# Eight 32x32 tiles in two PSUM banks for the last 26 keys of an attention, and one division for a whole unit

## The chip, the cores and the metric

One core of one Trainium2 chip runs the whole program. The metric is the device time of one execution in microseconds (us); 2626.75 us is the median of three runs of the kernel before.

## The reference

Four layers follow each other over an input of 4 batches of 1024 rows of 256 values. Each layer is a cross attention to 154 context rows ("keys"), then a feed-forward part. The attention of layers 1 to 3 has 16 heads of 16 values; layer 0 calls the same kind of attention with the layer's normalised rows as queries, feature maps of 32 values a head and its own output weight.

```python
x = x + tanh(g_xattn[l]) * xattn_l(layernorm(x), ctx_1024, ...)
x = x + tanh(g_ffn[l]) * ffn_l(layernorm(x), ...)
# inside an attention
scores = einsum('bhqd,bhkd->bhqk', q, k) / sqrt(d_k)
attn = softmax(scores, axis=-1)
x = einsum('bhqk,bhkd->bhqd', attn, v)
```

The feed-forward parts are a butterfly network folded into two matrices (layer 0), a linear layer with a top-2 low-rank choice (1), a ternary network with quantised activations (2) and a gated mixture with low-rank experts (3).

## The kernel before

The rows of a batch are cut into four blocks of 256; a stream `s` (0 to 3) takes one block through all layers, so that four independent streams share the engines. One attention of one stream in one layer `l` and batch is called a unit here: there are 16 units of layer 0 and 48 of layers 1 to 3. Every engine works through a fixed list of stages. A planner in the kernel (`orders`) makes the five lists: for each turn it takes the stream that a table of digits names (`TURN`, one string for each engine), and uses a cost for each stage (`parts`) to give out PSUM banks and to find gaps of TensorE of over 0.9 us, into which it puts `fill` matmuls that compute nothing (L982).

PSUM has 8 banks of 128 partitions x 512 fp32 values. Banks 0 to 3 form `quad`, for the scores. Banks 4 to 7 are handed out one at a time; `take(k)` makes TensorE wait until the engine that last read bank `k` is done.

The stages of a unit that matter here, in their order, each with its TensorE lines:

- `sc` and `mx` find the row maxima (L1136 to L1149), `mt` turns them.
- `st` (layer 0, L1175 and L1178) and `sts` (the others, L1196 and L1198) give the transposed scores of the last 26 keys, whose exponentials ScalarE writes to `s.Et`, which is stored in the buffers `xn` and `xT`. Layer 0 has two `st`, one for each half unit `u`, of one bank each.
- `s2` (L1219, L1222) and `ex` (ScalarE, L1585) give the exponentials `ET` of the first 128 keys, for one half unit at a time.
- `pv` multiplies them with the values. Its helper `through` does 8 matmuls of 128 keys (L1239, four column tiles of 32) and then 8 of the last 26 keys (L1247, 32x32 tiles whose row group and column group have the same number, into one bank). In layer 0 `pz` does the same with ones in place of the values, into a second bank: these are the sums of the softmax. In layers 1 to 3 the sums stand in unused columns of the values.
- `no` and `nz` divide: VectorE transposes the bank in 32x32 blocks (L1859), takes reciprocals (L1876) and transposes these back, spread over their heads (L1878); ScalarE copies the bank (L1601); GpSimd multiplies (L924) and adds (L926). All of it is done once for each half unit.
- `out` multiplies with the output weight (L1288).

```python
for q in range(4):
    t = e.matmul(bank[G4[q], 256 * z:256 * z + 256], last(z, q), Et[G4[q], 256 * a:256 * a + 256],
                 start=False, stop=True, skip_group_check=True)
```

Of the kernel before, what the change touches and what calls it, by code (L numbers as in the profile page):

```python
# [29 lines left out]
def build(nc, d, out):  # L30
# [5 lines left out]
    with ctx:  # L36
# [11 lines left out]
        ones = sb("ones", [128, 128])  # L48
# [130 lines left out]
        for i in range(NS):  # L179
# [3 lines left out]
            s.xn = sb(f"xn{i}", [128, 2, 256])  # L183
            s.xT = sb(f"xT{i}", [128, 2, 256])
# [6 lines left out]
            s.z = sb(f"z{i}", [128, 16])  # L191
# [41 lines left out]
            s.Et = [s.flat, xTf]  # L233

# [3 lines left out]

            s.PW = [s.flat, gu[:, 2048:2560], part(1536, [512])]
# [11 lines left out]

        def xrows(s, b):
            return slice(1024 * b + 256 * s.i, 1024 * b + 256 * s.i + 256)
# [3 lines left out]
        def parts(name, of):  # L257
            l = of[2] if name in ("qp", "sc", "s2", "ex", "pv", "pz", "no", "nz", "out", "split") else 0
            u = of[-1] if name in ("ex", "no") else 0
            key0 = name == "key" and of[1] == 0  # L260
            pe = {"grow": (150, 150, 250, 450, 880, 880, 880)[of[-1]] if name == "grow" else 0, "near": 450, "upt": 560, "tsum": 110, "key": 600 if key0 else 1150, "val": 1500, "turn": 600,
                  "qp": 910 if l == 0 else 1830, "sc": (740, 980, 740, 1280)[l], "mt": 220, "st": 1200,
                  "sts": 2500 if name == "sts" and of[2] == 3 else 1600, "s2": (1400, 1400, 1400, 2300)[l], "pv": 2000,
                  "pz": 2000, "out": 3550 if l == 0 else 1850, "up": 1800, "down": 7050, "gate1": 2150, "tl": 350,
# [3 lines left out]
                   "val": 850, "norm": 1750, "mx": 1390, "no": 1800 if l == 0 else 750, "nz": 950, "out": 770,  # L268
# [4 lines left out]
                   "turn": 600, "qp": 600 if l == 0 else 760, "mt": 350, "st": 500, "sts": 1100, "ex": 1800, "pv": 560,  # L273
                   "up": 860, "gate1": 200, "gate3": 200, "tl": 400, "q1": 500, "gelu2": 4400, "q2": 1000, "rd": 2400, "mw": 600,
                   "h1": 360, "h2": 360, "norm": 1000, "no": 900}
            pool = {"split": 1500, "key": 1500, "mw": 1650, "norm": 2600, "bias": 1550, "hw": 2050,
                    "no": 1250, "nz": 2350}
# [5 lines left out]
                   "split": "G", "no": "dg" if l == 0 else "Da", "nz": "dg", "pv": "PA" if l == 0 else "P",  # L283
# [11 lines left out]
        ONE = ("tsum", "key", "val", "turn", "qp", "mt", "st", "sts", "pv", "pz", "out", "up", "down", "gate1", "tl", "q1", "w1",  # L295
               "q2", "w2", "gate3", "mw", "exa", "h1", "f3")
        READ = {"tern": "DVE", "key": "ACT", "val": "DVE", "turn": "ACT", "qp": "ACT", "mt": "ACT", "st": "ACT", "sts": "ACT", "no": "DVE", "out": "DVE",
# [3 lines left out]
        def takes(name, of, engine):  # L301
# [4 lines left out]
            if (name, engine) == ("mw", "POOL") and of[1] == 0:  # L306
                return ["gated"]
            if engine == "PE" and (name in ONE or name == "back" and of[1] == 0):
# [1949 lines left out]
```

## Time and profile before

| | before |
|---|---|
| median of 3 runs | 2626.75 us (2623.39 to 2628.63) |
| profiled execution, span | 2625.2 us (no other time of it is listed) |
| TensorE busy | 2472.9 us, 94% |
| VectorE, ScalarE, GpSimd busy | 57%, 46%, 45% |
| TensorE's share of the chain that ended last | 74% |
| granted TensorE clock, mean | 0.992 |
| DMA | mean 14 GB/s |

The span is from the first to the last instruction. A fp32 matmul leaves two records in the trace, a bf16 matmul one, so 8 fp32 matmuls are "x16". The names are those of the program's buffers.

### The profile page before, as it was taken

To read this page: it belongs to the slowest core of one execution; us is meant where nothing else is said; L and a number is where in the kernel's file an instruction comes from. 1 tells how busy PE (TensorE), PEld (TensorE's weight loads), DVE (VectorE), ACT (ScalarE), POOL (GpSimd) and SP (SyncE) were. 2 spreads that over 40 slices of the span, in tenths; PEclk is the share of its full clock that TensorE was granted. 3 is DMA by queue.
4 is the path that set the end of the run, shared out by engine and by line. 5 is a ranking of instruction groups with operands and counts; after the bars stand their busy time and mean duration, and the time that the engine had idled before them with its cause. 6 is when DMAs were issued, how large, how long until landed. Compare 5 with 4: busy or idle time off the path is not lost.

```text
span 2625.2 us, 53630 instructions
## 1 busy us (share of the span) xinstructions
PE 2472.9 (94%) x21300; PEld 1670.9 (64%) x21300; DVE 1491.8 (57%) x3948; ACT 1204.5 (46%) x1930; POOL 1170.3 (45%) x2521
## 2 busy tenths in 40 slices
PE   8999888999999988899999998899999999889998
PEld 5676445777776644577777655467767765447776
DVE  7555787545433687754543467874543257876442
ACT  5535477322244547723224546762322545674221
POOL 2334644545343554444533355444534345545442
PEclk9999999999999999999999999999999999999999
DMA  3200100000000000000000000000000000000000
GB/s 130 84 12 12 76 14 2 1 9 9 9 9 12 12 1 14 2 6 12 1 9 20 1 12 1 12 1 9 9 9 9 12 1 12 1 1 1 5 5 9
DMA packets 16279, 37.37 MB, mean 14 GB/s; under 512 B 1408, under 2 KB 11424, under 8 KB 15008
## 3 DMA queue, kind: packets, MB, share of 16 engines
q1 hardware_dynamic: 16032, 33.94, 3.7%
q8 instruction: 172, 2.82, 0.5%
q14 instruction: 75, 0.61, 0.1%
HBM read 29.74 MB, written 4.19 MB: 13 GB/s over the span
## 4 chain that ended last, share of the span: by engine, by line
PE 74%; DVE 14%; ACT 5%; POOL 4%; issue 3%; DMA 0%; DVEq 0%; POOLq 0%; ACTq 0%
PE P L1431 8%; PE P L1239 4%; PE P L1247 4%; PE P L1140 4%; PE P L1464 4%; PE P L1440 4%; PE P L1449 4%; PE P L1313 4%; PE P L1432 4%; PE P L1300 4%; PE P L1288 4%; PE P L1219 4%; DVE mx L1849 4%; ACT ET L1585 2%; PE P L1109 2%
## 5 line engine op out<-in xcount | busy, mean ns | idle before, releaser
L1849 DVE TENSOR_REDUCE mx<-P 128x8 f32<-128x1232 f32 x256 | 367.7, 1436 | 195.8 <-PE P L1136 63.5
L872 POOL TENSOR_SCALAR sm<-sm 128x1 f32<-128x1 f32 x512 | 174.6, 353 | 457.9 <-DVE sm L1845 457.4
L1431 PE MATMUL P<-xT,w 128*128 128x256 f32 x1024 | 265.6, 382 | 1.5 <-DVE sm L2042 0.8
L1543 ACT ACTIVATE xn<-x,sm 128x256 f32<-128x256 f32 x256 | 139.5, 593 | 228.3 <-POOL sm L878 228.2
L1885 DVE SCALAR_TENSOR_TENSOR x<-P,w_first,x 128x512 f32<-128x512 f32 x96 | 71.9, 749 | 290.7 <-PE P L1465 109.1
L1431 PEld LDWEIGHTS P<-xT,w 128*128 128x128 f32 x1024 | 190.3, 190 | 51.7 <-issue 25.9
L1585 ACT ACTIVATE ET<-P 128x2048 f32<-128x2048 f32 x96 | 180.1, 1876 | 68.1 <-PE P L1222 46.4
L1663 ACT ACTIVATE gu<-P 128x256 f32<-128x256 f32 x128 | 49.0, 383 | 331.1 <-PE P L1432 311.0
L1140 PE MATMUL P<-KB,R 32*128 32x308 f32 x1536 | 156.5, 476 | 39.0 <-ACT ET L1585 16.2
L2072 DVE SCALAR_TENSOR_TENSOR gu<-gu,P 128x256 f32<-128x256 f32 x128 | 53.7, 419 | 215.9 <-ACT gu L1663 215.6
L1219 PE MATMUL P<-R,KB 32*128 32x256 f32 x2048 | 162.3, 403 | 8.3 <-DVE mx L1849 8.3
L1239 PE MATMUL P<-ET,VB 128*32 128x256 f32 x2048 | 137.0, 385 | 20.4 <-ACT ET L1585 15.2
L1432 PE MATMUL P<-gu,b 128*128 128x256 f32 x512 | 152.3, 379 | 0.0
L889 POOL TENSOR_TENSOR x<-x,w_bias 128x512 f32<-128x512 f32 x112 | 142.0, 1271 | 18.8 <-ACT xn L1543 18.8
L924 POOL TENSOR_TENSOR xT<-xT,R 128x512 f32<-128x512 f32 x48 | 61.0, 1272 | 184.3 <-DVE xT L1878 113.4
L877 POOL TENSOR_SCALAR sm<-sm 128x1 f32<-128x1 f32 x512 | 132.0, 272 | 24.5
L1440 PE MATMUL P<-gu,b 128*128 128x256 f32 x512 | 133.8, 384 | 0.0
L1140 PEld LDWEIGHTS P<-KB,R 32*128 32x128 f32 x1536 | 62.1, 185 | 101.6 <-issue 59.0
L950 POOL TENSOR_TENSOR xn<-xn,gu 128x512 f32<-128x512 f32 x48 | 60.9, 1270 | 145.0 <-DVE xn L2079 143.8
L1300 PE MATMUL P<-xT,wup 128*128 128x256 f32 x512 | 124.1, 387 | 0.4 <-ACT R L1609 0.4
L1219 PEld LDWEIGHTS P<-R,KB 32*128 32x128 f32 x2048 | 81.3, 186 | 65.4 <-issue 34.4
L1464 PE MATMUL P<-w_w,R 128*128 128x256 f32 x512 | 116.6, 381 | 3.4 <-issue 3.0
(310 smaller groups left out, 5583.7 us busy)
## 6 DMA issues: line engine op xcount, KB each, us to landing
kvw<-in_wkv SPq DMA_DIRECT2D x12, 672.0 KB, 4.0
x<-in_x SPq DMA_DIRECT2D x16, 256.0 KB, 2.9
out<-x SPq DMA_DIRECT2D x16, 256.0 KB, 2.1
w<-in_w SPq DMA_DIRECT2D x2, 1024.0 KB, 6.3
w<-in_wexp SPq DMA_DIRECT2D x1, 1028.0 KB, 7.8
w_w<-in_wcon SPq DMA_DIRECT2D x1, 1024.0 KB, 10.1
w_w<-in_m3t SPq DMA_DIRECT2D x1, 1024.0 KB, 8.6
w<-in_w1q SPq DMA_DIRECT2D x1, 1024.0 KB, 10.6
```

The lines of the kernel that those rows point to most:

```text
L872: own(e.tensor_scalar(a[:, i:i + 1], y[:, i:i + 1], y[:, i:i + 1], hv[:, i:i + 1], ALU.mult, ALU.mult), 1)
L889: e.tensor_tensor(s.x[:], s.x[:], gb[:, k:k + 1, :].broadcast_to([128, 2, 256]), ALU.add).then_inc(s.g_x, 1)
L1140: t = e.matmul(quad[:, g, 0:2 * NK], s.QT[G4[g], u, rows], K[G4[g], 2 * u:2 * u + 2, :], start=True, stop=l == 2)
L1219: e.matmul(quad[:, g, cols], K[G4[g], j, 0:128], s.QT[G4[g], j if l == 0 else u, :], start=a == 0, stop=False, skip_group_check=True)
L1239: t = e.matmul(bank[G4[q], 256 * z:256 * z + 256], main(z, q), ET[:, g, 256 * a:256 * a + 256], start=z == 0, stop=False, skip_group_check ...
L1300: t = e.matmul(o[:, 256 * (j % 2):256 * (j % 2) + 256], wup[:, c, 128 * j:128 * j + 128], s.xT[:, c, :], start=c == 0, stop=c == 1)
L1431: e.matmul(o, wm[:, c, js], s.xT[:, c, :], start=n == c == 0, stop=False, skip_group_check=True)
L1432: t = e.matmul(o, bm[:, js], U[:, 2 * n, :], start=False, stop=False, skip_group_check=True)
L1440: t = e.matmul(P[:, k, 256 * n:256 * n + 256], bm[:, js], U[:, 2 * n + 1, :], start=False, stop=n == 1, skip_group_check=True)
L1464: e.matmul(o, s.G[:, j, rows], w2[:, j, :], start=j == 0, stop=False)
L1585: e.activation(ET[:].rearrange("p g c -> p (g c)"), quad.rearrange("p g c -> p (g c)"), ACT.Exp, bias=mb1[:, b:b + 1] if l == 1 else 0.0). ...
L1849: e.tensor_reduce(s.mx[:, i, :, 2 * u:2 * u + 2], quad[:, :, 0:2 * NK].rearrange("p g (a k) -> p g a k", a=2), AX.X, ALU.max).then_inc(q_d, 1)
```

## The change

- The exponentials of the last 26 keys lie in one buffer `s.Et` of 128 x 2 x 512, whose halves `xn` and `xT` now are. Instruction rows of the changed kernel therefore say `Et` for all three.
- `st` is one stage for the whole unit of layer 0, into two banks. For each `u`, eight tiles follow each other, four with row group = column group in the first bank (`z` = 0), four with the row group 2 further on in the second bank (`z` = 1).
- `last` writes the product of the last 26 keys in the same way: row group `q` for `z` = 0, `q ^ 2` for `z` = 1, always column group `q`. In layer 0, `pv` does values and ones side by side in the two banks, and `pz` is gone. In layers 1 to 3, `pv` of `u` = 0 does only the first 128 keys; `pv` of `u` = 1 does its own, and then the last 26 keys of both half units as one block of 16 matmuls. The two banks are taken at `u` = 0 and kept.
- The division is done once for a unit of layers 1 to 3: two transposes, two reciprocals and one transpose back, a scaled copy of one bank by ScalarE, a multiply-add of the other bank by VectorE, one multiply by GpSimd. Bias rows and value columns are laid out anew to suit.
- `both` joins two neighbouring banks in one instruction of ScalarE or VectorE.
- The strings of `TURN` are all new, and the planner's costs of the stages above too.

```diff
-            s.xn = sb(f"xn{i}", [128, 2, 256])
-            s.xT = sb(f"xT{i}", [128, 2, 256])
+            s.Et = sb(f"Et{i}", [128, 2, 512])
+            s.xn, s.xT = (s.Et[:, z, :].rearrange("p (a b) -> p a b", a=2) for z in range(2))
...
+        def both(k0, k1):
+            k0, k1 = sorted((k0, k1))
+            if k1 == k0 + 1:
+                return [(slice(0, 2), P[:, k0:k0 + 2, :])]
+            return [(slice(z, z + 1), P[:, k:k + 1, :]) for z, k in enumerate((k0, k1))]
...
-                "0323230023233232020102202102220102210000331000333101333021211212111021212302123023201321222032322013"
...
-            def nz(s, b, l, u):
-                t = s.Z[u]
-                e.wait_ge(s.d_o, C.up(s.d_o))
-                e.wait_ge(s.a_q, 13 * b + 3 * l + 3 + u)
-                e.tensor_tensor(t, t, s.VS, ALU.mult).then_inc(s.g_z, 1)
-                e.wait_ge(s.g_z, C.up(s.g_z))
-                e.tensor_tensor(s.OT[:, u, :], t[:, 0:256], t[:, 256:512], ALU.add).then_inc(s.g_p, 1)
+            def nz(s, b, l):
+                e.wait_ge(s.d_o, C.up(s.d_o, 2))
+                e.tensor_tensor(s.OT[:, 0:2, :].rearrange("p a b -> p (a b)"), s.Z[0], s.VS, ALU.mult).then_inc(s.g_p, 1)
                 C.up(s.g_p)
...
-            def st(s, b, u, k):
+            def st(s, b, k0, k1):
                 K = KT[0]
...
+                k0, k1 = sorted((k0, k1))
                 banks = take(k0), take(k1)
...
                 for u in range(2):
...
+                    eight = [(g, z, banks[z][G4[g ^ 2 * z], 256 * u:256 * u + 256]) for z in range(2) for g in range(4)]
+                    for g, z, o in eight:
+                        e.matmul(o, K[G4[g], 2 * u + z, :], s.QT[G4[g], 2 * u + z, :], start=u == 0, stop=False,
+                                 skip_group_check=True)
+                    for g, z, o in eight:
+                        t = e.matmul(o, selt[G4[g], 2 * u + z, :], s.MT[G4[g], :], start=False, stop=True, skip_group_check=True)
...
+            def last(s, l, u, z, o, of):
+
+                for q in range(4):
+                    r = G4[q ^ 2 * z]
+                    t = e.matmul(o[G4[q], :], of[r, :], s.Et[r, z, 256 * u:256 * u + 256], start=False, stop=True, skip_group_check=True)
                 return t
...
                 if l == 0:
...
+                    for z, o in enumerate(banks):
+                        main(s, 0, u, z, o[:, half[0]], lambda q, z=z: V[:, 8 * u + 4 * z + q, :], True)
+                        t = main(s, 0, u, z, o[:, half[1]], lambda q: ones[:, 0:32], False)
+                    t.then_inc(p_et, 1)
+                    if u == 0:
+                        e.wait_ge(s.a_e, s.e)
+
+                    for z, o in enumerate(banks):
+                        last(s, 0, u, z, o[:, half[0]], Vt[:, 2 * u + z, :])
+                    for z, o in enumerate(banks):
+                        t = last(s, 0, u, z, o[:, half[1]], one26[:])
                     t.then_inc(s.p_d, 1)
...
+                for z, o in enumerate(banks):
+                    t = main(s, l, u, z, o[:, half[u]], lambda q, z=z: V[:, 8 * u + 4 * z + q, :], u == 0)
+                t.then_inc(p_et, 1)
+                if u == 0:
+                    return
+                e.wait_ge(s.a_e, s.e)
+
+                for n in range(2):
+                    for z, o in enumerate(banks):
+                        t = last(s, l, n, z, o[:, half[n]], Vt[:, 2 * n + z, :])
+                t.then_inc(s.p_d, 1)
...
+            def no(s, b, l, k0, k1):
+
+                e.wait_ge(s.d_a, C.up(s.d_a, 2) - 1)
+                e.activation(s.VS, P[:, k0, :], ACT.Copy, scale=tm[:, 2:3]).then_inc(s.a_q, 1)
...
+                for n in range(2):
+                    e.reciprocal(z[:, :, n], s.Z[n].rearrange("p (b c) -> p b c", c=32)[:, :, 16 - 16 * n]).then_inc(d_own, 1)
                 e.wait_ge(d_own, C.up(d_own, 2))
-                e.transpose(t, s.z[:].unsqueeze(2).broadcast_to([128, 16, 32])).then_inc(s.d_o, 1)
+                e.transpose(s.Z[0], z.unsqueeze(3).broadcast_to([128, 16, 2, 16])).then_inc(s.d_o, 1)
+                e.wait_ge(s.a_q, 10 * b + 2 * l + 4)
+                e.scalar_tensor_tensor(out=s.VS, in0=P[:, k1, :], scalar=tm[:, 3:4], in1=s.VS, op0=ALU.mult,
+                                       op1=ALU.add).then_inc(s.d_o, 1)
```

The first place is TensorE in the first units of layer 0 of the kernel before: the second `st`, then `pv` and `pz` of one half unit.

```order
L1175 MATMUL P<-R,KT 32x256 x4
L1178 MATMUL P<-R,selt 32x256 x4
L1175 MATMUL P<-R,KT 32x256 x4
L1178 MATMUL P<-R,selt 32x256 x4
L1018 MATMUL P<-b,w_b1q 128x256 x2
L1136 MATMUL P<-KB,R 128x154 x8
L1239 MATMUL P<-ET,VB 32x256 x8
L1247 MATMUL P<-xn,VR 32x256 x8
L1239 MATMUL P<-ET,ones 32x256 x8
L1247 MATMUL P<-xn,one 32x256 x8
```

In the changed kernel TensorE has there one `st`, and further on one `pv` for the same half unit.

```order
L1173 MATMUL P<-R,KT 32x256 x8
L1176 MATMUL P<-R,selt 32x256 x8
L1173 MATMUL P<-R,KT 32x256 x8
L1176 MATMUL P<-R,selt 32x256 x8
L1016 MATMUL P<-b,w_b1q 128x256 x2
```

```order
L1134 MATMUL P<-KB,R 128x154 x8
L1236 MATMUL P<-ET,VB 32x256 x4
L1236 MATMUL P<-ET,ones 32x256 x4
L1236 MATMUL P<-ET,VB 32x256 x4
L1236 MATMUL P<-ET,ones 32x256 x4
L1243 MATMUL P<-Et,VR 32x256 x8
L1243 MATMUL P<-Et,one 32x256 x8
```

The number of matmuls is the same; those of the last 26 keys (L1247 before, L1243 now) stand in one block of 16 where two blocks of 8 stood, and the changes of tile shape between L1239 and L1247 are one in place of three.

The second place is TensorE in the first units of layer 1. Before, each half unit ends with its own block of the last 26 keys.

```order
L1300 MATMUL P<-xT,wup 128x256 x4
L1239 MATMUL P<-ET,VB 32x256 x8
L1247 MATMUL P<-xn,VR 32x256 x4
L1247 MATMUL P<-xT,VR 32x256 x4
L1087 MATMUL P<-ident,xn 128x128 x4
L1219 MATMUL P<-R,KB 128x256 x4
L1222 MATMUL P<-R,sel 128x256 x4
L1219 MATMUL P<-R,KB 128x256 x4
L1222 MATMUL P<-R,sel 128x256 x4
```

Now the first half unit has none, and the second has both.

```order
L1156 MATMUL P<-identb,R 128x128 x2
L1236 MATMUL P<-ET,VB 32x256 x8
L1217 MATMUL P<-R,KB 128x256 x4
L1220 MATMUL P<-R,sel 128x256 x4
L1217 MATMUL P<-R,KB 128x256 x4
L1220 MATMUL P<-R,sel 128x256 x4
L1107 MATMUL P<-Et,w_wq 128x256 x4
L1236 MATMUL P<-ET,VB 32x256 x8
L1243 MATMUL P<-Et,VR 32x256 x16
```

The block of 8 behind the first L1239 has moved behind the second one and joined the block there.

The third place is VectorE's division in layer 1, before for two half units and now for one unit.

```order
L1859 STREAM_TRANSPOSE R<-P 128x512
L1876 RECIPROCAL z<-R 128x8 x2
L1878 STREAM_TRANSPOSE R<-z 128x512
L1859 STREAM_TRANSPOSE xT<-P 128x512
L1876 RECIPROCAL z<-xT 128x8 x2
L1878 STREAM_TRANSPOSE xT<-z 128x512
```

```order
L1884 STREAM_TRANSPOSE R<-P 128x512
L1884 STREAM_TRANSPOSE Et<-P 128x512
L1900 RECIPROCAL z<-R 128x16
L1900 RECIPROCAL z<-Et 128x16
L1902 STREAM_TRANSPOSE R<-z 128x512
L1904 SCALAR_TENSOR_TENSOR R<-P,w_first,R 128x512
```

Both transposes of PSUM now stand together, one transpose back is gone, and a multiply-add out of PSUM has come behind it. Over the whole program the lists hold 296 `fill` matmuls before and 309 now; GpSimd has 144 tensor-tensor instructions less, ScalarE 160 activations less and 2 table loads more.

## Rows read from the trace of the kernel before

**Rows 1.** The page: busy time by engine, and the chain that ended last.

```profile
PE 2472.9 (94%) x21300; PEld 1670.9 (64%) x21300; DVE 1491.8 (57%) x3948; ACT 1204.5 (46%) x1930; POOL 1170.3 (45%) x2521
PE 74%; DVE 14%; ACT 5%; POOL 4%; issue 3%; DMA 0%; DVEq 0%; POOLq 0%; ACTq 0%
```

**Rows 2.** Busy time by stretch, first and last of four equal stretches.

```profile
100.00:700.00 600.00, 562.55 (x5017) 377.39 (x5016) 357.03 (x934) 287.70 (x450) 269.63 (x594) 0.99 0.05 16
...
1900.00:2500.00 600.00, 571.38 (x5043) 384.75 (x5035) 338.67 (x900) 277.63 (x438) 269.23 (x575) 1.00 0.02 6
```

**Rows 3.** Timeline of TensorE, layer 0, `st`: start, duration, instruction, records.

```profile
70.47 0.63 PE L1175 MATMUL P<-R,KT 32*32 32x256 f32 x8
70.92 0.29 PE L1178 MATMUL P<-R,selt 32*32 32x256 bf16 x4
71.03 0.61 PE L1175 MATMUL P<-R,KT 32*32 32x256 f32 x8
71.47 0.29 PE L1178 MATMUL P<-R,selt 32*32 32x256 bf16 x4
71.68 0.71 PE L1219 MATMUL P<-R,KB 32*128 32x256 f32 x8
```

**Rows 4.** Timeline of TensorE, layer 0, `pv` and `pz` of one half unit.

```profile
75.37 1.07 PE L1239 MATMUL P<-ET,VB 128*32 128x256 f32 x16
76.37 1.06 PE L1247 MATMUL P<-xn,VR 32*32 32x256 f32 x16
77.36 1.07 PE L1239 MATMUL P<-ET,ones 128*32 128x256 f32 x16
78.36 1.07 PE L1247 MATMUL P<-xn,one 32*32 32x256 f32 x16
79.36 0.71 PE L1219 MATMUL P<-R,KB 32*128 32x256 f32 x8
...
80.66 3.72 PE L1288 MATMUL P<-w_fcw,R 128*128 128x256 f32 x16
84.22 0.60 PE L1087 MATMUL P<-ident,xn 128*128 128x128 f32 x4
```

**Rows 5.** Timeline of TensorE, layer 2, both `pv` of one unit.

```profile
351.04 1.07 PE L1239 MATMUL P<-ET,VB 128*32 128x256 f32 x16
...
360.52 1.07 PE L1239 MATMUL P<-ET,VB 128*32 128x256 f32 x16 [0.63 <-ACT ET L1585]
361.52 0.63 PE L1247 MATMUL P<-xn,VR 32*32 32x256 f32 x8
361.98 0.61 PE L1247 MATMUL P<-xT,VR 32*32 32x256 f32 x8
362.51 0.80 PE L1140 MATMUL P<-KB,R 32*128 32x308 f32 x8
```

**Rows 6.** Groups of TensorE: records, busy us and mean ns, idle before.

```profile
L1239 PE MATMUL P<-ET,VB 128*32 128x256 f32 x2048 | 137.0, 385 | 20.4 <-ACT ET L1585 15.2 <-issue 4.1
L1247 PE MATMUL P<-xn,VR 32*32 32x256 f32 x1024 | 77.9, 385 | 0.0
L982 PE MATMUL P<-identb 128*128 128x512 bf16 x296 | 77.7, 389 | 4.5 <-POOL mg L839 4.5
```

**Rows 7.** Groups of the division and the residual, on the other engines.

```profile
L1859 DVE STREAM_TRANSPOSE R<-P 128x512 f32<-128x512 f32 x48 | 34.2, 713 | 24.0 <-PE P L1247 24.0
L1878 DVE STREAM_TRANSPOSE R<-z 128x512 f32<-128x512 f32 x48 | 34.1, 711 | 1.7
L1885 DVE SCALAR_TENSOR_TENSOR x<-P,w_first,x 128x512 f32<-128x512 f32 x96 | 71.9, 749 | 290.7 <-PE P L1465 109.1 <-PE P L1313 98.5 <-PE P L1288 78.4
L1876 DVE RECIPROCAL z<-R 128x8 f32<-128x8 f32 x96 | 13.1, 178 | 1.0
L1601 ACT ACTIVATE R<-P,w_first 128x256 f32<-128x256 f32 x192 | 80.3, 472 | 80.6 <-DVE R L1859 42.6 <-DVE xT L1859 33.8 <-POOL R L924 3.8
L924 POOL TENSOR_TENSOR R<-R 128x512 f32<-128x512 f32 x48 | 60.9, 1269 | 68.4 <-DVE R L1878 42.3 <-ACT R L1601 26.1
L926 POOL TENSOR_TENSOR R<-R 128x256 f32<-128x256 f32 x48 | 35.0, 728 | 3.8
```

More of the change, by code:

```diff
@@ L307, in takes @@
                 return ["gated"]
+            if (name, engine) == ("pv", "PE") and of[2] > 0 and of[3] > 0:
+                return []
             if engine == "PE" and (name in ONE or name == "back" and of[1] == 0):
-                return ["bank"] * (2 if name in ("sts", "gate1") else 1)
+                return ["bank"] * (2 if name in ("st", "sts", "gate1", "pv") else 1)
             return []
@@ L314, in gives @@
                 return ["quad"]
-            if engine == "PE" and (name == "pz" or name == "pv" and of[2] > 0):
+            if (name, engine) == ("pv", "PE"):
                 return ["ET"]
-            if (name, engine) == ("pv", "ACT") or (READ.get(name) if name != "no" or of[2] == 0 else "ACT") == engine:
-                return ["bank", "gated"] if name == "e3" else ["bank"] * (2 if name in ("sts", "lin") else 1)
+            if (name, engine) in (("pv", "ACT"), ("nz", "DVE")) or READ.get(name) == engine and (name != "no" or of[2]):
+                return ["bank", "gated"] if name == "e3" else ["bank"] * (2 if name in ("st", "sts", "lin", "pv") else 1)
             return []
@@ L627, in build @@
+            "SP": "0300030102300000123000001230002103",
         }
@@ L1193, in sts @@
                 for u in range(2):
-                    o = [banks[g // 2][64 * (g % 2):64 * (g % 2) + 64, 256 * u:256 * u + 256] for g in range(4)]
+                    o = [banks[g // 2][64 * h:64 * h + 64, 256 * u:256 * u + 256] for g, h in enumerate((0, 1, 1, 0))]
                     for g in range(4):
@@ L1851, in mx, with pv, no @@
                 C.up(q_d)
-            def no(s, b, l, u, k):
-                t, bank = s.Z[u] if l else s.Et[u], P[:, k, :]
+            def pv(s, b, l, u, k0, k1):
+                e.wait_ge(s.p_d, C.up(s.p_d))
+                for z, of in both(k0, k1):
+                    t = e.transpose(s.Et[:, z, 256 * u:256 * u + 256], of[:, :, 256:512])
+                t.then_inc(s.d_a, 1)
+                C.up(s.d_a)
+            def no(s, b, l, *at):
                 C.up(s.g_p)
-                e.wait_ge(s.p_d, C.up(s.p_d))
@@ L1858, in no @@
                 if l:
[L1859 to L1860 removed]
+                    e.wait_ge(s.p_d, C.up(s.p_d))
+                    for z, k in enumerate(at):
+                        e.transpose(s.Z[z], P[:, k, :]).then_inc(s.d_a, 1)
+                    C.up(s.d_a, 2)
                     return
[L1862 to L1864 removed]
```

318 lines of the change are left out of this document (147 added, 171 removed).

## The prediction, before the changed kernel had run

> **What bounds the kernel now.** I read the page first. TensorE is busy for 2472.9 of 2625.2 us, no other engine for more than 57%, and TensorE has 74% of the chain that ended last [rows 1]. Then the stretches: between 100 and 2500 us TensorE is busy for 563 to 571 of every 600 us [rows 2], so it is idle for 29 to 37 us in each. The kernel is bound by TensorE, evenly, with about 152 us of idle time in all (2625.2 - 2472.9). Some of the busy time is not work: 77.7 us are `fill` matmuls, which stand where the planner expects a gap [rows 6]. A microsecond of real TensorE work that goes away is a microsecond of time, as long as the gaps don't grow.
>
> Last I read the timeline of the stages that are changed, by the starts of the pieces, since the ends overlap. A block of 8 fp32 matmuls of the last 26 keys (L1247, 16 records) runs from 76.37 to 77.36, 1.00 us; the block of the 128 keys ahead of it (L1239) takes 1.00 us as well [rows 4]. What is in that microsecond? Two blocks of one tile shape that follow each other show it: the second L1175, 8 records, takes 71.47 - 71.03 = 0.44 us, and the first L1178, 4 records, 0.11 us [rows 3]. Full-array fp32 matmuls of 256 columns take 3.56 us for 16 records [rows 4], 0.22 us each. So four records of 32x32 tiles together take what one full-array record takes: the four tiles run at the same time, in groups of 0.216 us. A block of 16 records is four such groups, 0.864 us, and 0.136 us for the change of tile shape.
>
> **The change part by part.** The price of a block now hangs on one question: do the four tiles of the second bank run beside the four of the first? They have row groups of their own kind in the order (`q ^ 2`), so all eight tiles are different ones. No row shows eight tiles at once. The nearest rows on one side are the four at once of L1247; on the other, L1219, 32x128 tiles, four row groups that write all columns of four banks: its 8 records last 0.71 us in all, with the drain [rows 3], where one at a time would need 8 x 0.216 = 1.73 us. There the whole array is at work at once, and each column group serves four row groups; nothing in the rows forbids eight 32x32 tiles in two banks. The bounds are 1.03 us for 32 records, if all eight overlap, and 1.86 us (8 groups and a change of shape), if the second bank's four wait. I take full overlap: a group of eight records costs 0.216 us, and I allow 0.03 us a block for the four more starts. A block of 32 records is then 4 x 0.216 + 0.136 + 0.03 = 1.03 us.
>
> - Layers 1 to 3, last 26 keys: two blocks of 1.00 us [rows 4, 5] become one of 1.03: 0.97 us less, 48 units: 46.6 us.
> - Layer 0, last 26 keys: `pv` and `pz` of a half unit, 2 x 1.00, become one block of 1.03. Two half units in each of 16 units: 32 x 0.97 = 31.0 us.
> - Layer 0, the 128 keys: two blocks of 1.00 us now follow each other, one change of shape less: 32 x 0.136 = 4.4 us.
> - `st`: one stage is 71.68 - 70.47 = 1.21 us [rows 3], two are 2.42 us. The new one has the same four pieces, each of eight tiles: 1.21 + 0.03 = 1.24. Saved 1.18 x 16 = 18.9 us.
> - `sts`, `s2`, `sc`: the same tiles and counts, nothing.
>
> The sum is 100.9 us of TensorE work less, 4%.
>
> **The other engines.** In layers 1 to 3 GpSimd did 1.27 + 0.73 us for each half unit and now does 1.27 once: 2.73 us less a unit, 131 us over 48. ScalarE did four copies of 0.47 and does one of twice the width, between 0.47 and 0.94; at 0.6 it is 4 x 0.47 - 0.6 = 1.28 a unit, some 60 us less. VectorE loses a transpose of 0.71 and gets a multiply-add of 0.75 [rows 7]: nothing. So none of them comes nearer to being the bound. What gets longer is the tail of a unit, from TensorE's last product to `out`: before 0.71 + 2 x 0.18 + 0.71 + 1.27 + 0.73 = 3.8 us, now 2 x 0.71 + 0.36 + 0.71 + 0.75 + 1.27 = 4.5 us [rows 7]. Behind it waits `out` of that stream and everything that TensorE has in its list behind `out`. It costs nothing while the three other streams' work stands between; that cover is the 9.5 us between the two `pv` of a unit, which is other streams' work too [rows 5]. If it were gone everywhere it would cost 0.7 x 48 = 34 us. The new `last` block also waits for nothing that was not there: `s.Et` is older by a half unit than before.
>
> **The gaps.** By its code the planner fills 0.6 of a gap that it expects, and counts 0.215 us for a fill matmul. 13 more of them mean 13 x 0.215 / 0.6 = 5 us more of expected gaps. That is the only trace of the new order in numbers, and I add 5 us. 2626.75 - 100.9 + 5 = 2530.9; the span of the profiled execution is 1.6 us under the median and would give 2529. I say 2530 us.
>
> **A rule against it.** Four tiles of L1247 lie in four row groups and write one bank, and they take 0.216 us together [rows 3, 4]. The Trainium skill, TensorEngine Tiling (Array Packing), Restrictions and Gotchas, says that different row tiles can't access the same PSUM bank at the same time. Taken as it stands, the 16 records of a block before would need 16 x 0.216 = 3.5 us and the 32 now at least that. The row of 1.00 us contradicts it for tiles that also differ in their column group, as all do within one bank here. The same skill, TensorE: Matmul & The Clock Gate, Part 3, tells of 16 tiles of 32x32 at 10.6 times the speed of one; no row here shows more than four 32x32 tiles.
>
> **The rivals.** (a) *The second bank's tiles wait for the first's.* Each column group then serves one tile at a time. For it speaks that no row has two tiles of one column group in flight at this tile size; against it, L1219, where four row groups share all columns. Then only changes of shape are saved: 0.136 us for 80 joined blocks, 4.4 us in the 128 keys, 0.1 us for each of 16 `st`: 17 us, so 2626.75 - 17 + 5 = 2615 us. (b) *They overlap by half*: the second four start one record late, since a matmul's second record queues ahead of them. A block then needs five groups in place of four, and so does each piece of `st`: 0.216 x (80 + 32) = 24 us back: 2555 us. (c) *The waits take part of it*: the longer tail at its full 34 us, or waits for a bank: 2545 to 2590, about 2565 us. (d) *Slower: banks.* In layers 1 to 3 two of the four single banks are now held from the first `pv` to the multiply-add: in the unit shown, 9.5 us between the `pv` [rows 5] plus 1.0 + 1.0 + 3.2, about 15 us, where one bank was held for a few us at a time. Two units that overlap hold all four, and every `take` behind them (`turn`, `qp`, `mt`, `up`) stands until VectorE is through. It decides from 101 / 48 = 2.1 us a unit; at 3 us it gives 2530 + 144 = 2674 us. For it speaks that TensorE's list can't go around a stage that waits; against it, that the planner hands out these same banks and would have shown such waits as gaps, hence as fills, and there are only 13 more. (e) *The new order is better by itself*, with idle time down by 20 us or more: 2505 us.
>
> **How the numbers follow.** Forecast 0.68, (a) 0.05, (b) 0.07, (c) 0.12, (d) 0.03, (e) 0.05. A measurement of this kernel can't tell less than about 0.2%, 5 us, from no change; every case but (d) is faster by more, and I leave 0.01 for no change, between (a) and (d). Faster 0.96, same 0.01, slower 0.03. The forecast's own spread is the gaps, -15 to +20 us: 2515 to 2550. The range takes in (b), the lower half of (c) and part of (e): 2510 to 2560 us.
>
> **What the profile of the changed kernel would show.** L1243: a block of 32 records from start to the next line's start in about 1.03 us (1.25 with (b), 1.9 with (a)), and a busy time for each 1024 records of about half of the 77.9 us that they have now [rows 6]. L1173 with 16 records in about 0.46 us. TensorE busy at about 2375 us, the idle time at 150 to 160 us. GpSimd busy some 130 us less. If idle time is at 190 us or more, with L1236 or the stages behind a `take` waiting for VectorE's multiply-add, (c) or (d) is at work. I am wrong if the block takes much over 1.1 us, or if the waits before `out` and `take` have grown by more than 20 us.

## The result: less than half of the forecast gain

The changed kernel takes 2584.66 us (median of 4 runs, 2579.62 to 2586.76), the kernel before 2625.97 us (4 runs, 2623.39 to 2628.63) on the same chip. The ratio is 0.9839, 95% interval [0.9824, 0.9853]: 41 us faster, where 97 were forecast. 2584.66 lies outside the forecast's 2510 to 2560 us. The profiled execution of the changed kernel took 2586.76 us, its span is 2585.0 us and its mean granted TensorE clock 0.980; before, the clock was 0.992 over 2625.2 us.

The page of the changed kernel, busy time and chain, answers to [rows 1]. The third row is the granted clock in 40 slices, in tenths; before the change all 40 digits were 9.

```profile
PE 2398.4 (93%) x21282; PEld 1654.5 (64%) x21313; DVE 1451.4 (56%) x3871; ACT 1162.8 (45%) x1772; POOL 1036.9 (40%) x2377
...
PEclk9999899999999999999999988999999999899999
...
PE 69%; DVE 15%; ACT 7%; issue 5%; POOL 4%; DMA 1%; SPq 0%; DVEq 0%; POOLq 0%; ACTq 0%
```

By this page TensorE is busy 74.5 us less (forecast 98), and idle for 186.6 us in place of 152.3; 6.5 us of both are not real, as the ledger below says. TensorE's share of the chain fell from 74% to 69%; ScalarE's and "issue" grew. GpSimd is busy 133 us less, as forecast (130). ScalarE has 42 us less (60 forecast): the old copies overlapped, 192 of 0.472 us in 80.3 us [rows 7], the new ones take 0.68 us each, and there are two table loads more. VectorE has 40 us less (nothing forecast); it is spread over many small groups, and its cause was not looked for.

The timeline of TensorE, for layer 0 and for layer 2, answers to [rows 3 to 5]: start, duration, instruction, records, idle time before.

```profile
48.06 0.66 PE L1173 MATMUL P<-R,KT 32*32 32x256 f32 x16
48.51 0.31 PE L1176 MATMUL P<-R,selt 32*32 32x256 bf16 x8
...
55.94 0.61 PE L1236 MATMUL P<-ET,ones 128*32 128x256 f32 x8
56.48 0.66 PE L1243 MATMUL P<-Et,VR 32*32 32x256 f32 x16
56.94 0.64 PE L1243 MATMUL P<-Et,one 32*32 32x256 f32 x16
57.51 0.71 PE L1217 MATMUL P<-R,KB 32*128 32x256 f32 x8
```

```profile
359.01 0.80 PE L1138 MATMUL P<-KB,R 32*128 32x308 f32 x8 [0.84 <-ACT R L1583]
359.74 1.07 PE L1236 MATMUL P<-ET,VB 128*32 128x256 f32 x16
360.74 1.09 PE L1243 MATMUL P<-Et,VR 32*32 32x256 f32 x32
361.76 0.61 PE L980 MATMUL P<-identb 128*128 128x512 bf16 x2
```

Read the starts. The 32 records of L1243 take 361.76 - 360.74 = 1.02 us, and 57.51 - 56.48 = 1.03 us in layer 0: all eight tiles run at once. L1173 with 16 records takes 48.51 - 48.06 = 0.45 us, as 8 records did. So TensorE does have what the sum said. The time is not there.

**The ledger.** Where did it go? I split each span into three: the idle time of the page (span less PE's busy time); what the lower clock costs, (1 - granted clock) x span; and the rest, TensorE's work at full clock, fills included. The middle term is exact only if TensorE works all through a stretch at half clock; in the changed kernel it was busy for 92 of 102 us of such stretches. The ratio of each run is to runs of the kernel before that were made beside it. Each split is that of the kernel's own profiled execution.

Nine of these traces lack records of TensorE. The page shows it: 21282 matmuls beside 21313 weight loads in the changed kernel, where the kernel before has 21300 of both. All 31 are missing from one group, which has 128 records in e3 and e4:

```profile
L1388 PE MATMUL P<-w1i,Et 128*128 128x512 bf16 x97 | 33.2, 399 | 9.2 <-ACT Et L1648 4.8 <-issue 2.2 <-ACT R L1583 0.5
```

A block of two such records lasts 0.59 us and a single one 0.38, so each missing record takes 0.21 us out of "work" and puts it into "idle": 6.5 us for 31. The table has the numbers of the pages as they are, and the last column says how many records are missing; the text below puts the 6.5 us back (5 us in e6). With that, after, e4, e5 and e9, whose work is the same, agree within 3 us, and before and e6 within 6.

| kernel | time, ratio to before | span | work | clock | idle | missing records |
|---|---|---|---|---|---|---|
| before | 2625.97 | 2625.2 | 2451.9 | 21.0 | 152.3 | 0 |
| after | 2584.66, 0.9839 | 2585.0 | 2346.7 | 51.7 | 186.6 | 31 |
| e1 before, bf16 halves | 2584.94, 0.9836 | 2579.7 | 2349.1 | 38.7 | 191.9 | 0 |
| e2 after, bf16 halves | 2548.33, 0.9698 | 2545.2 | 2303.4 | 40.7 | 201.1 | 0 |
| e3 after, four at a time | 2642.42, 1.0056 | 2640.0 | 2436.8 | 29.0 | 174.2 | 0 |
| e4 after, short tail | 2569.45, 0.9778 | 2569.1 | 2353.7 | 41.1 | 174.3 | 0 |
| e5 after, short norm | 2540.45, 0.9668 | 2537.2 | 2345.7 | 27.9 | 163.6 | 31 |
| e6 before, short norm | 2597.14, 0.9882 | 2595.0 | 2440.9 | 18.2 | 135.9 | 24 |
| e7 after, no fills | 2605.59, 0.9915 | 2602.2 | 2274.9 | 80.7 | 246.6 | 31 |
| e8 after, 0.9 filled | 2576.31, 0.9801 | 2580.2 | 2385.7 | 43.9 | 150.6 | 31 |
| e9 after, norm in pairs | 2565.6, 0.977 | 2563.8 | 2348.4 | 33.3 | 182.1 | 31 |
| e10 after, bf16, 0.9 filled | 2552.17, 0.9718 | 2548.8 | 2336.6 | 38.2 | 174.0 | 30 |
| e11 e10 and pairs | 2539.09, 0.9667 | 2538.5 | 2333.0 | 43.2 | 162.3 | 30 |
| e12 e2 and short norm | 2506.3, 0.9537 | 2502.4 | 2291.7 | 35.0 | 175.7 | 30 |

After against before, with the missing records put back: work -99 (forecast -101), clock +31 (not forecast), idle +28 (forecast +5).

**The clock.** The term that was not forecast can be read in one place. The timeline of TensorE and the granted clock (the last but two numbers of a window's row) around 1590 us of the changed kernel:

```profile
1577.40 0.61 PE L1195 MATMUL P<-R,KT 32*64 32x256 f32 x8
1577.84 0.29 PE L1197 MATMUL P<-R,selt 32*64 32x256 bf16 x4
...
1583.98 0.71 PE L1217 MATMUL P<-R,KB 32*128 32x256 f32 x8 [0.46 <-DVE mx L1868]
...
1587.41 0.80 PE L1138 MATMUL P<-KB,R 32*128 32x308 f32 x8 [2.06 <-ACT ET L1608]
1588.14 1.36 PE L1236 MATMUL P<-ET,VB 128*32 128x256 f32 x16
1589.43 1.96 PE L1243 MATMUL P<-Et,VR 32*32 32x256 f32 x32
1592.98 0.61 PE L1353 MATMUL P<-ident,R 128*32 128x128 f32 x2 [1.60 <-ACT R L1622]
...
1600.08 1.07 PE L1195 MATMUL P<-R,KT 32*64 32x256 f32 x8
1600.93 0.43 PE L1197 MATMUL P<-R,selt 32*64 32x256 bf16 x4
```

```profile
1575.00:1588.00 13.00, 10.06 (x126) 5.81 (x124) 9.46 (x35) 5.26 (x5) 3.45 (x9) 1.00 0.00 0
1588.80:1602.50 13.70, 10.21 (x83) 4.14 (x80) 9.38 (x29) 4.21 (x8) 5.75 (x13) 0.50 0.00 1
1603.00:1616.00 13.00, 10.67 (x94) 6.21 (x87) 8.09 (x28) 12.10 (x13) 6.08 (x20) 1.00 0.00 0
```

TensorE waited 0.46 us for VectorE's row maxima (L1217, at 1583.98) and then 2.06 us for ScalarE's exponentials, and at 1588.8 us the clock fell to 1.2 GHz (0.50) for 13.7 us. The same block of L1195 takes 0.44 us ahead of it and 0.85 us in it. The Trainium skill, TensorE: Matmul & The Clock Gate, Part 1, gives 1.2 GHz for the "cold" array, its lower level, at which matmuls follow each other at half the pace; these rows agree. The kernel before has a like place at 1616 to 1630 us: TensorE waited for 1.03 us for the row maxima and then 1.87 us for the exponentials, with five fills in between where the changed kernel has none, and was busy for 9.90 of the 14 us. The clock stayed at 1.00. So waits of this length come before the fall, but they don't always bring it.

What is such a term worth in time? Executions of one and the same kernel differ in their clock. Of the 32 executions of the kernel before that were made beside e1 to e12, one had a clock of 0.993 and 2622.47 us, another 0.987 and 2635.42: 13 us for a clock term that differs by 16. A line through all 32 gives 0.76 us of span for each us of the term; 54 executions of the other kernels, each against the mean of its own, give 0.59. By that estimate the 31 us are worth 18 to 23 us of time. It is an estimate, because the gaps of these executions are not known.

### The profile page after: what moved, and what is told of

It reads as the page before. It is cut to its first block, busy times and chain, and to the rows that moved or that the text cites. A ratio compares the mean times of both kernels' runs of the same rounds, so it can differ in the third digit from the quotient of the medians.

```text
span 2585.0 us, 53036 instructions
## 1 busy us (share of the span) xinstructions
PE 2398.4 (93%) x21282; PEld 1654.5 (64%) x21313; DVE 1451.4 (56%) x3871; ACT 1162.8 (45%) x1772; POOL 1036.9 (40%) x2377
## 4 chain that ended last, share of the span: by engine, by line
PE 69%; DVE 15%; ACT 7%; issue 5%; POOL 4%; DMA 1%; SPq 0%; DVEq 0%; POOLq 0%; ACTq 0%
PE P L1451 9%; PE P L1484 4%; PE P L1236 4%; PE P L1452 4%; PE P L1469 4%; PE P L1460 4%; PE P L1333 4%; PE P L1217 4%; DVE mx L1868 4%; PE P L1320 4%; PE P L1138 4%; PE P L1308 3%; ACT ET L1608 3%; PE P L1243 2%; PE P L1107 2%
## 5 line engine op out<-in xcount | busy, mean ns | idle before, releaser
L873 POOL TENSOR_SCALAR sm<-sm 128x1 f32<-128x1 f32 x512 | 170.9, 344 | 520.0 <-DVE sm L1864 519.6
L1451 PE MATMUL P<-Et,w 128*128 128x256 f32 x1024 | 264.5, 381 | 0.3 <-DVE gu L2093 0.3
L1451 PEld LDWEIGHTS P<-Et,w 128*128 128x128 f32 x1024 | 191.7, 190 | 54.7 <-issue 26.1
L1563 ACT ACTIVATE Et<-x,sm 128x256 f32<-128x256 f32 x256 | 139.2, 593 | 182.7 <-POOL sm L879 182.6
L923 POOL TENSOR_TENSOR R<-R 128x512 f32<-128x512 f32 x48 | 61.2, 1274 | 323.2 <-DVE R L1904 323.1
L1217 PE MATMUL P<-R,KB 32*128 32x256 f32 x2048 | 171.4, 422 | 4.2 <-DVE mx L1868 4.1
L1236 PE MATMUL P<-ET,VB 128*32 128x256 f32 x2048 | 146.0, 391 | 23.0 <-ACT ET L1608 12.4
L1452 PE MATMUL P<-gu,b 128*128 128x256 f32 x512 | 152.3, 379 | 0.0
L1217 PEld LDWEIGHTS P<-R,KB 32*128 32x128 f32 x2048 | 85.3, 195 | 63.3 <-issue 39.3
L1320 PE MATMUL P<-Et,wup 128*128 128x256 f32 x512 | 124.8, 389 | 0.0
L947 POOL TENSOR_TENSOR Et<-Et,gu 128x512 f32<-128x512 f32 x48 | 60.9, 1269 | 155.2 <-DVE Et L2106 155.2
```

Of the source, the lines that this page charges most:

```text
L873: own(e.tensor_scalar(a[:, i:i + 1], y[:, i:i + 1], y[:, i:i + 1], hv[:, i:i + 1], ALU.mult, ALU.mult), 1)
L1217: e.matmul(quad[:, g, cols], K[G4[g], j, 0:128], s.QT[G4[g], j if l == 0 else u, :], start=a == 0, stop=False, skip_group_check=True)
L1236: t = e.matmul(o[G4[q], :], of(q), ET[:, g, 256 * a:256 * a + 256], start=start, stop=False, skip_group_check=True)
L1320: t = e.matmul(o[:, 256 * (j % 2):256 * (j % 2) + 256], wup[:, c, 128 * j:128 * j + 128], s.xT[:, c, :], start=c == 0, stop=c == 1)
L1451: e.matmul(o, wm[:, c, js], s.xT[:, c, :], start=n == c == 0, stop=False, skip_group_check=True)
L1452: t = e.matmul(o, bm[:, js], U[:, 2 * n, :], start=False, stop=False, skip_group_check=True)
```

## The experiments

Theory A, the prediction's own: TensorE bounds, so that its work is worth its full time, and what was missed came in with the new order, the longer tail or the banks. Theory B: the chains of the four streams through VectorE, GpSimd and ScalarE bound part of the time, so that TensorE's work is worth less than its time in any order. Theory C: gaps lower TensorE's clock, and that costs a part. Ratios are those of the table; intervals stand with each run.

**e1: TensorE's saving alone, in the kernel before.** Order, banks, tail and the other engines stay.

```diff
-    t = e.matmul(bank[G4[q], 256 * z:256 * z + 256], last(z, q), Et[G4[q], 256 * a:256 * a + 256],
+    hi = lambda x: x.bitcast(bf16).rearrange("p (n h) -> p n h", h=2)[:, :, 1]
+    t = e.matmul(bank[G4[q], 256 * z:256 * z + 256], hi(last(z, q)), hi(Et[G4[q], 256 * a:256 * a + 256]),
```

> The kernel before, its order, its banks and its division untouched; only the matmuls of the last 26 keys (L1247) read the upper halves of the fp32 numbers as bf16, so the numbers lose digits. TensorE work: a block of 16 records of 0.216 us by fours becomes 8 records of 0.109 us by fours, 0.65 us less for each of 160 blocks, 103 us less in all, about what the change took away. Theory A (TensorE work is worth its full time; the new order, the longer tail or the held banks gave the gain back): about 2523 us. Theory B (TensorE work is worth less than half of its time, because gaps open between the stages of four streams, whatever the order): 2575 to 2590 us.

Measured: [0.9816, 0.9856], 42 us less, for 103 us less work in the ledger. The page and a block in layer 0:

```profile
PE 2387.8 (93%) x20020; PEld 1630.2 (63%) x20020; DVE 1491.4 (58%) x3948; ACT 1201.9 (47%) x1930; POOL 1166.6 (45%) x2521
```

```profile
73.41 0.41 PE L1248 MATMUL P<-xn,VR 32*32 32x256 bf16 x8
73.75 1.07 PE L1239 MATMUL P<-ET,ones 128*32 128x256 f32 x16
```

The block is down from 1.00 to 0.34 us, the other engines have the busy times of before [rows 1], and idle time is up by 40 us, the clock's share by 18. Nothing but TensorE's work was taken, and it was worth 0.41 of its time. This is the run that decides against A's first half. The time is that of the changed kernel, but this doesn't show that order, tail and banks cost nothing: e3 bears on that.

**e2: the same edit in the changed kernel**, on its line 1243.

> The changed kernel with the same bf16 reading in its block of the last 26 keys (L1243): 0.65 us less for each of 80 blocks, 52 us less TensorE work, no instruction moved. Theory A: about 2533 us. Theory B: some 20 us less than the changed kernel, 2560 to 2570 us.

Measured: [0.968, 0.9717], 36 us less than after. Both blocks of layer 0 (first and last start: 57.57, 57.92) now take 0.35 us in place of 1.03:

```profile
57.57 0.31 PE L1244 MATMUL P<-Et,VR 32*32 32x256 bf16 x8
57.70 0.29 PE L1244 MATMUL P<-Et,one 32*32 32x256 bf16 x8
57.92 0.71 PE L1217 MATMUL P<-R,KB 32*128 32x256 f32 x8
```

80 blocks x 0.68 are 54 us of work (the ledger shows 50), for 36 us of time: 0.67 of it. That is neither theory's time: A had 2533 us, B 2560 to 2570. TensorE's work is worth less than its time here too, but more than the 0.41 of the kernel before.

**e3: the second bank's tiles on the row groups of the first.** Each tile of the array is used by both banks; the values change, the counts don't.

```diff
-    eight = [(g, z, banks[z][G4[g ^ 2 * z], 256 * u:256 * u + 256]) for z in range(2) for g in range(4)]
+    eight = [(g, z, banks[z][G4[g], 256 * u:256 * u + 256]) for z in range(2) for g in range(4)]
...
-    r = G4[q ^ 2 * z]
+    r = G4[q]
```

> The changed kernel with the four tiles of the second bank put back on the row groups of the first bank's (row group = column group), in st and in last, so that values are multiplied with the wrong rows in the second bank, and only four tiles can run at once. If the eight tiles really overlap by the tile's place alone, a block of the last 26 keys goes from 1.03 to 1.86 us and st gains four times two groups: 80 x 0.84 + 16 x 1.08 = 84 us more TensorE work. Theory A: about 2669 us. Theory B: 2610 to 2640 us. If the overlap does not hang on the row group: 2585 us.

Measured: [1.0034, 1.0079], 58 us over after for 84 us more work, 0.69 of it; 2642.42 us is just above B's range.

```profile
57.97 1.07 PE L1243 MATMUL P<-Et,VR 32*32 32x256 f32 x16
58.86 1.04 PE L1243 MATMUL P<-Et,one 32*32 32x256 f32 x16
59.83 0.50 PE L1217 MATMUL P<-R,KB 32*128 32x256 f32 x4
```

The block takes 59.83 - 57.97 = 1.86 us, rival (a)'s price to the hundredth. So the overlap of eight is real, it needs eight different tiles, and it is worth 58 us of the changed kernel's time. With more to do, TensorE has 6 us less idle time and 23 us less of the clock's share.

e3 is also the changed kernel without the eight at once, the kernel that rival (a) priced at 2615 us: new order, held banks, longer tail and lighter GpSimd, with TensorE's saving down to the changes of tile shape (forecast 17 us, 15 in the ledger). It took 2642 us. It is slower than the kernel before by 16 us, clear of noise, with 22 us more idle time and 8 more of the clock's share. So of the 55 us by which the forecast of 2530 us was missed, some 28 are there already without the eight at once (2642 against 2615), and some 26 come with it (84 us less work for 58 us of time). Of the 22 us, 12 stand in front of one stage, the one that transposes the factors of layer 1's low-rank choice. These are waits of TensorE: us in total, times, longest. First the kernel before, then the changed one.

```profile
PE P L1333 <- DVE R L1950: 3.7, 4, 1.6
PE P L1333 <- ACT R L1601: 1.9, 2, 1.6
PE P L1333 <- DVE x L1885: 0.5, 1, 0.5
```

```profile
PE P L1353 <- DVE R L1977: 11.4, 10, 2.1
PE P L1353 <- ACT R L1622: 4.0, 3, 1.6
PE P L1353 <- ACT R L1583: 2.8, 3, 0.9
```

That is 6.1 us before and 18.2 us after. It is 18.2 us in e3 as well, and 7.8 us in e1, whose order is the old one.

**e4: a shorter tail.** The second bank's transpose and the multiply-add work on a part of their columns; the values change.

```diff
-    e.transpose(s.Z[z], P[:, k, :]).then_inc(s.d_a, 1)
+    w = 32 if z else 512
+    e.transpose(s.Z[z][:, 0:w], P[:, k, 0:w]).then_inc(s.d_a, 1)
...
-    e.scalar_tensor_tensor(out=s.VS, in0=P[:, k1, :], scalar=tm[:, 3:4], in1=s.VS, op0=ALU.mult,
+    e.scalar_tensor_tensor(out=s.VS[:, 0:8], in0=P[:, k1, 0:8], scalar=tm[:, 3:4], in1=s.VS[:, 0:8], op0=ALU.mult,
```

> The changed kernel with VectorE's part of the tail of a unit in layers 1 to 3 cut short: the second transpose is of 32 columns and the multiply-add of 8, and both reciprocals read the first bank, so the second half of the heads is divided by wrong sums and mostly not added. VectorE's chain behind TensorE's last product falls by 1.2 to 1.4 us in each of 48 units, below that of the kernel before. If the longer tail or the banks that it holds gave the gain back: 20 to 35 us less, 2550 to 2565 us. If the tail lies beside other streams' work: within 5 us of 2585 us.

Measured: [0.9758, 0.9797], 15 us less than after. The edit took less than the expectation says: the transpose went from 0.67 to 0.17 us and the multiply-add from 0.71 to 0.19, 1.03 us a unit, and VectorE is busy 46 us less. The tail isn't covered, but not at its full price either: 15 us for some 49 (48 x 1.03). The 0.74 us a unit that the change added then cost about 15 x 0.74 / 1.03 = 11 us, an estimate.

**e5 and e6: the chains alone.** One of the two Newton steps in each of the 128 norms on GpSimd is left out, in the changed kernel and in the kernel before. TensorE's list is untouched.

```diff
-    for n in range(2):
+    for n in range(1):
...
-    own(e.tensor_scalar(y[:, i:i + 1], a[:, i:i + 1], (R_1, R_3)[n], y[:, i:i + 1], ALU.add, ALU.mult), 1 - i * n)
+    own(e.tensor_scalar(y[:, i:i + 1], a[:, i:i + 1], (R_1, R_3)[n], y[:, i:i + 1], ALU.add, ALU.mult), 1 - i)
```

> The changed kernel with one of the two Newton steps of each normalisation's inverse square root left out, so that it is less exact. GpSimd does six small operations less, about 1.8 us, in each of 128 normalisations; ScalarE, the turn on TensorE and all that follows in that stream wait for them. TensorE's work is unchanged. Theory A (TensorE alone bounds): within 5 us of 2585 us. Theory B (the streams' own chains through the other engines set a part of the time): 20 to 50 us less, 2535 to 2565 us.

> The same step left out of the kernel before. Theory B says that the chains weigh less the more TensorE work lies beside them, so the gain is smaller than that of the changed kernel: 10 to 30 us less, 2597 to 2617 us. If the chains weigh as much as there, the time is 20 to 50 us less; if TensorE alone bounds, none.

Measured: e5 [0.9648, 0.9687], 44 us less than after; e6 [0.9864, 0.9901], 30 us less than before. The page of e5:

```profile
PE 2373.6 (94%) x21282; PEld 1646.2 (65%) x21313; DVE 1447.4 (57%) x3871; ACT 1161.4 (46%) x1772; POOL 825.4 (33%) x1609
```

An engine that is busy for 40% loses work, and the kernel gains as much as from the whole change. In the ledger, e5's work is that of after, its idle time 23 us less and the clock's share 24 us less. Who waits for these instructions stands in two rows of after, idle time in front and its releaser at the end:

```profile
L1563 ACT ACTIVATE Et<-x,sm 128x256 f32<-128x256 f32 x256 | 139.2, 593 | 182.7 <-POOL sm L879 182.6
L873 POOL TENSOR_SCALAR sm<-sm 128x1 f32<-128x1 f32 x512 | 170.9, 344 | 520.0 <-DVE sm L1864 519.6
```

VectorE's sums release GpSimd, GpSimd releases ScalarE, and TensorE turns what ScalarE made. GpSimd is busy 1.65 us less a norm (211.5 us in e5, 216.1 in e6, over 128 norms), so 1.65 x 128 / 4 = 53 us of each stream's own time went; 30 of them counted before the change and 44 after it. So the chains bound part already before, and a larger part afterwards.

**e7 and e8: the fills.** The share of an expected gap that is filled goes from 0.6 to nothing, and to 0.9.

```diff
-    lists["PE"].append(("fill", let["bank"][0][1], int(0.6 * (at - free["PE"]) / 215.0)))
+    lists["PE"].append(("fill", let["bank"][0][1], int(0.9 * (at - free["PE"]) / 215.0)))
```

> The changed kernel with no fill matmul at all (309 before), nothing else moved. The granted clock of TensorE was 0.980 with them. Theory C (a good part of the loss is the clock, which falls after gaps): the clock falls to 0.95 or lower and the time rises by 20 to 60 us. If the clock is not what costs: within 5 us of 2585, or a little faster, since no fill delays a stage.

> The changed kernel with fills for 0.9 in place of 0.6 of each gap that the planner expects, some 460 fill matmuls. Theory C: the clock goes back to about 0.99, TensorE's low spells from 104 us to 50 or less, and the time falls by 10 to 25 us, to 2560 to 2575. If the fills reach over the gaps, they delay the stages behind them: 2585 to 2610 us.

Measured: e7 [0.9892, 0.9939], 21 us more than after; e8 [0.9779, 0.9824], 8 us less (10 by the ratios, whose intervals just touch). The 309 fills of after are 72 us of "work" that does nothing, and taking them out costs 21 us: idle time rises by 60 and the clock's share from 52 to 81 us. The direction is theory C's, the sizes are not: without fills it expected a clock of 0.95 or lower and got 0.969; with more fills it expected 2560 to 2575 us and low stretches of 50 us or less, and got 2576 us and 91 us of them, in the slowest of four executions (their clocks: 0.983, and 0.986 to 0.987 in the others).

**e9: a shorter norm with the same arithmetic**, both columns in one instruction.

```diff
-    for i in range(2):
-        own(e.tensor_scalar(a[:, i:i + 1], y[:, i:i + 1], y[:, i:i + 1], hv[:, i:i + 1], ALU.mult, ALU.mult), 1)
+    own(e.tensor_tensor(a, y, y, ALU.mult), 0)
+    own(e.tensor_tensor(a, a, hv, ALU.mult), 0)
...
-    for i in range(2):
-        own(e.tensor_scalar(y[:, i:i + 1], a[:, i:i + 1], (R_1, R_3)[n], y[:, i:i + 1], ALU.add, ALU.mult), 1 - i * n)
+    own(e.tensor_scalar(w, a, (R_1, R_3)[n], None, ALU.add), 0)
+    own(e.tensor_tensor(y, w, y, ALU.mult), 0)
```

> The changed kernel with the square root of the layer norm on GpSimd written for both columns at once: seven tensor_tensor of 128x2 and three tensor_scalar of 128x2 in the place of ten tensor_scalar of 128x1, the same arithmetic. By the changed kernel's rows a norm goes from 4 x 0.344 + 4 x 0.269 + 2 x 0.266 = 2.98 us to some 7 x 0.197 + 3 x 0.27 = 2.19 us of GpSimd time (the 0.27 is an estimate, from the 128x1 form with numbers as operands), and each instruction now waits for the one before it. TensorE's work is the same. Theory A (TensorE alone bounds, chains are hidden): no change, 2580 to 2588 us. Theory B (the four streams' chains through the other engines bound part of the time): one Newton step less took 1.8 us a norm and 44 us, so 0.5 to 0.8 us a norm gives 12 to 20 us: 2565 to 2573 us. If the waits eat the gain, no change, and that says nothing on A or B unless GpSimd's time of a norm did fall.

Measured: [0.9756, 0.9785], 19 us less than after, near the largest gain that theory B allowed. GpSimd is busy for 935.7 us, 101 less, 0.79 us a norm. It computes what after computes, and is faster than both kernels.

**e10, e11, e12: the edits together.**

> The changed kernel with two edits that ran apart before: the last 26 keys' products of all layers read the upper halves of the numbers as bf16 (36 us less by itself, in a call of its own), and nine tenths of the planned gaps filled with idle matmuls in the place of six tenths (8 us less by itself). Which digits the products have changes with the first. Theory C (part of what was missed is TensorE's slower clock after gaps): bf16 makes the gaps longer, so that fills are worth as much here or more: 2535 to 2541 us, and fewer stretches at half clock than the 84 us or so of the changed kernel. Theory B alone: fills are worth nothing more once TensorE has less to do: 2545 to 2550 us.

> All three edits together: bf16 halves in the last 26 keys' products, nine tenths of the gaps filled, and the norm's square root for both columns at once. If the three are worth what they are worth apart: 36 + 8 + 12 to 20 us less than the changed kernel's 2585, so 2520 to 2530 us. By theory B the chain's cut is worth more once TensorE has less to do: at the lower end of it. By theory A: as the run before, with no gain from the norm.

> The changed kernel with two edits that ran apart before: one Newton step less in each of the 128 norms on GpSimd (44 us less by itself) and the last 26 keys' products on bf16 halves (36 us less by itself, of some 52 us of TensorE work); it leaves out the second Newton step and, in those products, the lower halves of the numbers. Theory B (streams' chains bound part of the time; where they are shorter, TensorE bounds more of it and its work is worth more of its time): the 52 us of TensorE work are worth more than their 36 here, 42 to 52 us: 2488 to 2498 us. If instead the two edits shorten the same chains (bf16 also takes time from the chain itself, a block of eight tiles 0.7 us), the second is worth as much or less: 2504 to 2512 us. Under theory A alone (TensorE alone bounds) the norm would have been worth nothing, which has fallen.

Measured: e10 [0.9704, 0.9733], 4 us over e2 (the intervals overlap) in place of the 7 to 13 less that C expected. More fills are worth nothing beside the bf16 halves: idle time falls by 34 us, and the work, fills included, grows by 40. (The changed kernel's stretches at half clock come to 104 us; the 84 of the expectation are e2's.) e11 [0.9652, 0.9683], 13 us less than e10, but not the 2520 to 2530 of a plain sum; the chain's cut was worth less beside the other edits (13 us) than alone (19), where B expected more. e12 [0.9515, 0.9558], 34 us less than e5 and 42 less than e2: the two edits add up (36 and 44 apart), so TensorE's work did not become worth more where the chains are shorter. That is the weaker of theory B's two readings, the one in which both edits shorten the same chains.

## Why the prediction was wrong

- **The question of eight tiles, the block of 1.03 us:** right, and not by luck: e3 is its control. 1.02 and 1.03 us measured, `st` 0.45 against 0.46. With the tiles no longer different ones, e3 gives rival (a)'s 1.86 us. The rule from the Trainium skill, TensorEngine Tiling (Array Packing), Restrictions and Gotchas, by which row tiles can't access the same bank at the same time, does not hold here: four row groups, each with a column group of its own, write one bank within 0.22 us.
- **The sum, 100.9 us of TensorE work less:** right, 99 by the ledger. GpSimd's 131 us: 133.
- **"A microsecond of real TensorE work that goes away is a microsecond of time, as long as the gaps don't grow":** this is the step that failed, with its number for the gaps, +5 us. The gaps grew by 28 and TensorE's clock, which the prediction left out, cost 31 us more in the ledger. The span missed the forecast's 2529 by 55.7 us: 30.7 (clock) + 22.8 (27.8 - 5.0, gaps) + 2.2 (work). In the kernel before, with nothing else changed, the same cut of work brought 42 of 103 us (e1); in the changed kernel, 84 us of it are worth 58 (e3).
- **Why the gaps grow, first:** 94% busy [rows 1] was read as "bound by TensorE", and the waits at its other 152 us as a fixed remainder. They are places where a stream's chain through the other engines is later than TensorE. Take time from TensorE, and more of those places come up: 40 us in e1. I argued that none of the other engines comes nearer to being the bound, from their busy time; e5, e6 and e9 show that a chain needs no busy engine to bound: it is made of latencies, one engine after the other.
- **Why the gaps grow, second:** by e3, 22 of the 28 us and 8 of the clock's 31 come with the rest of the change, before the eight tiles run at once. So e1's account is not the whole one: a cut of 103 us opens 40 us of gaps in the old order, and one of 84 us, from e3 to after, 6 us in the new one. No run takes the order, the banks and the tail apart, so what part each has stays open; the tail has an estimate below, from e4, and the banks have their waits.
- **The gaps' number:** it was taken from the planner's fills, 13 more. The planner's own expected gaps did not foretell what the chip waits: 13 fills went with 28 us.
- **The tail "costs nothing":** about 11 us, estimated from e4. That is rival (c)'s mechanism with a third of its price. Rival (c)'s time, 2545 to 2590, held the result, and had 0.12; its cause was mostly another one.
- **Rival (d), banks:** seen, but small. The two held banks come free with ScalarE's scaled copy (L1622) and VectorE's multiply-add (L1904). In the changed kernel TensorE's matmuls waited 7.9 us for the first (before L1353 and L1085, which take such a bank) and 0.5 us for the second, in e3 almost the same; before, it was 1.9 us for the copies (L1601). That is some 6 of the 28 us, where (d) needed 100.
- **Rival (e), the new order is better by itself:** not seen. With order, banks, tail and lighter GpSimd together, e3 is 16 us slower than the kernel before, although it has 15 us less TensorE work. Which of them costs it wasn't tried.
- **The signs of being wrong did not show it.** The block took 1.03 us. The waits before `out` are 6.4 us (L1308), 3.0 before (L1288), and those for the held banks some 6 us more, where 20 us more were set as the sign. Idle time is 180 us, above the 150 to 160 expected and under the 190 that were named as a sign. The clock was in no sign.

What stays open is how the clock's 31 us and the gaps' 28 us share the blame. The fall at 1588.8 us followed waits, and e8 and e9 lower the clock's share by 8 and 18 us. The spread between executions says that about 0.6 to 0.8 of the clock's share is time; no run here holds the gaps fixed and changes the clock.

## What to carry to other kernels

A kernel with an engine at 94% is not bound by it alone. Before costing a cut on the busiest engine at its full time, take the idle time that it has left, ask what ends each wait, and price the cut at the share that is not given back; here it was 0.4 in the old order and 0.7 in the new one. And build the kernel with all of the change but the saving itself (here e3): what it loses has another cause than the saving. The cheapest test is to shorten something small on an idle engine in the same chains (e6: 30 us from GpSimd alone): if the time moves, the busy engine isn't the only bound, and the chain's microsecond may be cheaper to win than TensorE's.

## What the runs showed of the hardware

- Eight 32x32 fp32 tiles that write two banks, each column group serving two row groups, take 0.22 us for one record each, as four tiles or one full-array record do. Two products on the same tile follow each other (1.86 us a block against 1.03).
- Matmuls read bf16 from every second 2-byte element (the upper half of fp32) without a visible price: a block of 16 records takes 0.35 us against 1.03 us for 32 in fp32, each group of eight some 0.11 us, as the bf16 records of L1178 do [rows 3].
- Two executions of the unchanged kernel before with granted clocks of 0.987 and 0.993 differ by 13 us.
- On GpSimd a tensor_tensor of 128x2 takes 0.20 us, a tensor_scalar of 128x2 with numbers as operands 0.22, and a tensor_scalar of 128x1 with operands from memory 0.34:

```profile
L873 POOL TENSOR_TENSOR sm<-sm 128x2 f32<-128x2 f32 x256 | 49.8, 195 | 533.2 <-DVE sm L1865 522.9
...
L878 POOL TENSOR_SCALAR sm<-sm 128x2 f32<-128x2 f32 x256 | 56.6, 221 | 22.5
```

These two rows are e9's, by group of GpSimd: records, busy us and mean ns. The 0.34 us are L873's of the changed kernel, above.
